# One decoder layer on one core: weight addresses worked out ahead, a shorter inverse root, and a redrawn timetable

## What is computed

```
x = layernorm(x + causal_linear_attention(x))      # 16 heads of 64, 128 random features, exp(x.W - |x|^2/2)
x = layernorm(x + differential_cross_attention(x, ctx))   # 32 half heads of 8, 77 context tokens
x = layernorm(x + experts(x))                      # 16 experts of 128, 4 chosen per token in 2 of 4 groups, and 1 shared
layernorm(x) = (x - mean) / sqrt(var + 1e-5)
```

## Time and profile before

| | |
|---|---|
| median of 3 runs | 789.55 us (783.31 to 789.67) |
| the profiled execution, its own time | 784.78 us |
| its span, from the first to the last instruction | 782.1 us |
| mean granted TensorE clock | 0.986 of full speed |
| PE busy | 731.6 us, 94% of the span |
| DVE busy | 546.0 us, 70% |
| ACT busy | 433.7 us, 55% |
| POOL busy | 273.8 us, 35% |

### The profile page before, as it was taken

How to read it: one execution, slowest core, us unless ns; L and a number is a source line. 1 busy time by engine, 2 the same in 40 slices (tenths; PEclk the granted TensorE clock), 3 DMA queues, 4 the chain that set the end, 5 groups by cost and what they waited for, 6 DMA issues and landing times.

```text
span 782.1 us, 24288 instructions
## 1 busy us (share of the span) xinstructions
PE 731.6 (94%) x9544; PEld 508.8 (65%) x9544; DVE 546.0 (70%) x1549; ACT 433.7 (55%) x880; POOL 273.8 (35%) x320
## 2 busy tenths in 40 slices
PE   5979999999999999999999999998799999999983
PEld 2547666756676776567667756776677787775643
DVE  8477755369546686865758599448989558943887
ACT  4867776264756534567565354753146766664331
POOL 7222112011232110625311054230265255556872
PEclk9999999999999999999999999999989999999997
DMA  8335676424000000311300041043686225424461
GB/s 281 141 95 155 189 149 162 126 54 127 2 3 2 3 2 19 120 41 45 95 2 3 2 156 55 9 165 136 210 272 188 64 92 171 147 82 161 141 208 56
DMA packets 55181, 80.78 MB, mean 103 GB/s; under 512 B 12576, under 2 KB 43424, under 8 KB 54560
## 3 DMA queue, kind: packets, MB, share of 16 engines
q1 hardware_dynamic: 48416, 62.71, 26.3%
q0 software_dynamic: 5376, 15.47, 5.1%
q10 hardware_dynamic: 1280, 1.05, 0.5%
HBM read 42.65 MB, written 33.41 MB: 97 GB/s over the span
## 4 chain that ended last, share of the span: by engine, by line
PE 65%; DVE 25%; issue 3%; ACT 2%; DMA 2%; SPq 1%; POOL 1%; ACTq 0%; DVEq 0%
PE ps L1657 28%; PE ps L1663 14%; PE ps L1755 7%; PE ps L1736 3%; PE ps L1880 3%; DVE xmax L1519 3%; PE ps L1771 3%; DVE st L1328 2%; DVE rows L1345 2%; PE ps L1799 1%; PE ps L1772 1%; DVE root_a L1337 1%; SPq L766 1%; PE ps L1944 1%; DVE attn_mem L1485 1%
## 5 line engine op out<-in xcount | busy, mean ns | idle before, releaser
L968 POOL TENSOR_TENSOR qk<-square,qk 128x512 f16<-128x512 f32 x64 | 75.8, 1186 | 258.9 <-ACT qk L1060 258.8
L1657 PE MATMUL ps<-x_split,w_qkv 128*128 128x512 f16 x384 | 93.8, 382 | 2.9 <-DVE qk L1481 1.9
L1663 PEld LDWEIGHTS ps<-attn_mem 128*64 128x64 f32 x1920 | 78.6, 138 | 24.0 <-issue 21.3
L1663 PE MATMUL ps<-attn_mem 128*64 128x65 f32 x1920 | 93.3, 226 | 0.3 <-issue 0.2
L990 POOL DMA_INDIRECT rows_out<-attn_mem,dest x64 | 62.5, 977 | 41.3 <-ACT attn_mem L1161 26.7
L983 POOL DMA_INDIRECT rows_in<-rows,slot_i x48 | 47.5, 989 | 73.3 <-DVE slot_i L1418 61.2
L1481 DVE SCALAR_TENSOR_TENSOR qk<-ps,qk 128x512 f16<-128x512 f32 x64 | 43.8, 684 | 41.8 <-ACT square L1057 41.6
L1063 ACT ACTIVATE attn_mem<-ps 128x512 f32<-128x512 f32 x64 | 37.7, 595 | 62.1 <-PE ps L1736 62.0
L1101 ACT ACTIVATE prob<-ps 128x512 f32<-128x512 f32 x96 | 52.9, 603 | 21.5 <-PE ps L1663 12.2
L1657 PEld LDWEIGHTS ps<-x_split,w_qkv 128*128 128x128 f16 x384 | 37.1, 98 | 37.7 <-issue 3.9
L1657 PE MATMUL ps<-attn_mem,w_qkv 128*128 128x128 f16 x512 | 55.8, 223 | 3.2 <-DVE attn_mem L1585 2.5
(11 more groups left out here) (307 smaller groups left out, 1872.7 us busy)
## 6 DMA issues: line engine op xcount, KB each, us to landing
attn_mem<-rows_in SPq DMA_DIRECT2D x64, 144.0 KB, 2.4
late_mem<-ffn_w SPq DMA_DIRECT2D x17, 384.0 KB, 3.6
rows_in<-zero_row SPq DMA_DIRECT2D x32, 144.0 KB, 4.8
up_split<-late_mem SPq DMA_DIRECT2D x16, 256.0 KB, 2.8
x_stage<-xT SPq DMA_DIRECT2D x4, 512.0 KB, 5.7
down_split<-late_mem SPq DMA_DIRECT2D x16, 128.0 KB, 2.8
rows<-x SPq DMA_DIRECT2D x4, 512.0 KB, 6.9
xq<-late_mem SPq DMA_DIRECT2D x32, 64.0 KB
```

Of the source, the lines that this page charges most:

```text
L968: pool.tensor_tensor(parts[:, 3, :], square[:, n % 2, :], parts[:, 2, :], ALU.subtract).then_inc(p_sql.sem, 1)
L1657: ins = pe.matmul(dst, lhs(i), rhs(j), start=first and n == 0, stop=last and n == 2)
L1663: ins = pe.matmul(dst[at:at + COLS, :], lhs[:, at:at + COLS], rhs, start=start, stop=stop)
```

## The change

Three things change.

1. PE works out weight addresses ahead of their use. "tile turn" loads the table and puts the 16 addresses of its pair's "tile up" weights on a list (`unaddressed`). After each product of `three_pass` outside "tile up", each transpose of "tile turn", each step of block 3's scores and each product of "probs", `address_ahead` takes one address from the list and has it computed. "tile up" drops what is left of its own and of earlier pairs and computes it where it is used. "tile down" forms its addresses as an expert's byte offset plus a base.
2. `inverse_root` has nine linked instructions instead of twelve: the shift is folded into the first guess, and two Newton steps of second order and third order stand for three of second order.
3. All constants of the timetable are new, the offsets of the engines and the bank holding times too.

```
-ATT = dict(project=(-2.394, -1.514), turn_keys=(2.018, 2.44), q_features=0.94, k_features=0.945,
+ATT = dict(project=(-2.397, -1.539), turn_keys=(2.004, 2.284), q_features=0.91, k_features=0.944,
...
-             dispatch=22.637, keep=35.532, ends=27.727, dispatch_d=0.271)
+             dispatch=22.919, keep=33.392, ends=29.062, dispatch_d=0.114)
...
-HOLD = dict(values=0.478, project=0.75, turn_keys=0.423, q_features=0.397, state=0.595, attend=0.594,
+HOLD = dict(values=0.615, project=0.705, turn_keys=0.635, q_features=0.453, state=0.572, attend=0.527,
...
-           sums_d=1.144, sums_n=0.742, early=-3.569, early_d=1.039, late=5.66, late_d=1.031, pack=-2.023)
+           sums_d=1.139, sums_n=0.634, early=-3.561, early_d=1.048, late=5.674, late_d=1.034, pack=0.189)
...
-    gpsimd=dict(project=0.29, weigh=-1.098, dispatch=-0.9, tile_down=-0.681, combine=-2.003, dense_keep=-0.444,
-                weigh_last=-2.512),
+    gpsimd=dict(project=0.53, weigh=-0.71, dispatch=-1.182, tile_down=-2.911, combine=-2.044, dense_keep=-0.39,
+                weigh_last=-4.65),
...
                 link(dve.tensor_scalar(v, mv[:, :, 1], LN_EPS, None, ALU.add))
-                link(dve.tensor_scalar(a.bitcast(I32), v.bitcast(I32), 1, None, ALU.logical_shift_right))
-                link(dve.tensor_scalar(r.bitcast(I32), a.bitcast(I32), -1.0, float(0x5F3759DF), ALU.mult, ALU.add))
-                for _ in range(3):
-                    link(dve.tensor_tensor(a, r, r, ALU.mult))
-                    link(dve.scalar_tensor_tensor(a, a, -0.5, v, ALU.mult, ALU.mult))
-                    link(dve.scalar_tensor_tensor(r, a, 1.5, r, ALU.add, ALU.mult))
+
+                link(dve.tensor_scalar(r.bitcast(I32), v.bitcast(I32), -0.5, float(0x5F3759DF), ALU.mult, ALU.add))
+
+                link(dve.tensor_tensor(a, r, r, ALU.mult))
+                link(dve.scalar_tensor_tensor(a, a, -0.5 * 0.375, v, ALU.mult, ALU.mult))
+                link(dve.scalar_tensor_tensor(r, a, 1.5 * 0.375, r, ALU.add, ALU.mult))
+                link(dve.tensor_tensor(a, r, r, ALU.mult))
+                link(dve.scalar_tensor_tensor(a, a, 64 / 9, v, ALU.mult, ALU.mult))
+                link(dve.scalar_tensor_tensor(a, a, -10 / 3, a, ALU.add, ALU.mult))
+                link(dve.scalar_tensor_tensor(r, a, 5.0, r, ALU.add, ALU.mult))
...
+            def byte_of(b, n, j, width):
+                return pe.snap(expert_of[b, n, j] * (2 * width))
+
+            def up_weights(b, n, j, part, k, a):
+                first = 2 * (D * k + P * part)
+                return e_bytes[a][:, bass.ds(byte_of(b, n, j, GU) + first, 2 * P)].bitcast(F16)
+
+            def down_weights(b, n, j, a):
+                return d_bytes[a][:, bass.ds(byte_of(b, n, j, D), 2 * D)].bitcast(F16)
+
+            def address_ahead():
+
+                if unaddressed:
+                    pe.lower_ap(unaddressed.popleft()(), for_matmul_weights=True)
+
+            def three_pass(dst, lhs, rhs, first=True, last=True, ahead=True):
 
                 for n, (i, j) in enumerate(((0, 0), (0, 1), (1, 0))):
                     ins = pe.matmul(dst, lhs(i), rhs(j), start=first and n == 0, stop=last and n == 2)
+                    if ahead:
+                        address_ahead()
                 return ins
...
+                    while unaddressed and unaddressed[0].args[1] <= n:
+                        unaddressed.popleft()
                     for j in range(2):
-                        at = pe.snap(expert_of[b, n, j] * (2 * GU))
                         for part in range(2):
                             for k in range(KD):
                                 m = KD * j + k
-                                first = 2 * (D * k + P * part)
                                 last = three_pass(bank[:, 2 * P * part + P * j:2 * P * part + P * j + P],
-                                                  lambda a: e_bytes[a][:, bass.ds(at + first, 2 * P)].bitcast(F16),
-                                                  lambda a: xgT[:, i % 3, a, P * m:P * m + P], k == 0, k == KD - 1)
+                                                  lambda a: up_weights(b, n, j, part, k, a),
+                                                  lambda a: xgT[:, i % 3, a, P * m:P * m + P], k == 0, k == KD - 1, False)
```

More of the change, by code:

```diff
@@ L1 @@
 import itertools
+from collections import deque
 from contextlib import ExitStack
+from functools import partial
 import numpy as np
@@ L117 @@
-MISC = dict(keys=3.411, tail=8.014, setup=1.455, setup_d=0.979, load_x=3.099, split_x=-4.602, load_stream=8.241,
-            experts_0=-6.556, experts_1=-3.498, rows_in=-2.106, up=1.797, down=4.371)
+ATT = dict(project=(-2.397, -1.539), turn_keys=(2.004, 2.284), q_features=0.91, k_features=0.944,
+           attend=(1.761, 3.758), state=(2.697, 3.71), output=(3.718, 4.667), turn_output=5.579, values_0=2.035,
+           values_1=0.095)
+CHAIN = dict(first=3.585, first_d=0.296, out=3.822, out_d=0.124, norm1=4.455, turn=5.065, queries=5.599, scores=6.487,
+             scores_d=0.077, maxima=9.427, probs=9.919, probs_d=0.118, norm2=13.642, cross=15.275, gate=15.822,
+             route0=16.089, up=16.389, route1=18.529, route2=19.696, down=17.08, route3=19.7, prefix=21.998,
+             dispatch=22.919, keep=33.392, ends=29.062, dispatch_d=0.114)
@@ new lines @@
+CHAIN_2 = dict(first=3.358, first_d=0.409, out=3.813, out_d=0.273, norm1=4.884, turn=5.611, queries=5.812,
+               scores=6.986, scores_d=0.055, maxima=9.324, probs=9.953, probs_d=0.115, norm2=14.088, cross=15.41,
+               gate=17.227, route0=17.235, up=18.013, route1=18.25, route2=19.181, down=19.566, route3=19.533,
+               prefix=20.058, dispatch=14.958, keep=19.669, ends=20.223, dispatch_d=0.309)
+HOLD = dict(values=0.615, project=0.705, turn_keys=0.635, q_features=0.453, state=0.572, attend=0.527,
+            turn_output=0.61, k_features=0.672, output=0.546, project_out=0.573, turn_stream=0.951, queries=0.819,
+            scores=0.631, turn_maxima=0.901, probs=0.551, weigh=0.666, turn_cross=1.378, gate=1.06, shared_up=1.569,
+            shared_down=2.669, prefix=0.578, pack=2.553, weights=0.756, tile_turn=1.201, tile_up=1.02,
+            tile_down=1.493, dense_gate=0.505, dense_up=2.697, dense_weigh=2.753)
@@ L121, in schedule @@
+MISC = dict(keys=6.832, tail=8.292, setup=0.909, setup_d=1.015, load_x=1.404, split_x=-3.754, load_stream=11.123,
+            experts_0=-7.69, experts_1=-5.301, rows_in=-1.611, up=1.751, down=4.284)
 def schedule():
@@ L218, in chain_jobs @@
             put(start + at["ends"], "table", 0, 1)
[L222 to L225, removed]
-           sums_d=1.144, sums_n=0.742, early=-3.569, early_d=1.039, late=5.66, late_d=1.031, pack=-2.023)
+END = dict(first=-4.562, first_d=0.943, out=-3.312, out_d=0.191, norm1=0.048, turn=-0.212, queries=0.274,
+           scores=-0.296, scores_d=0.244, maxima=7.759, probs=8.889, probs_d=0.137, norm2=16.756, cross=19.297,
+           gate=19.448, route0=19.786, up=21.87, route1=21.391, route2=22.532, down=23.756, route3=24.733,
+           weights=26.377, dense=26.844, dense_d=2.132, dense_2=1.336, pick=1.418, keep=1.879, sum=6.474, sums=36.876,
+           sums_d=1.139, sums_n=0.634, early=-3.561, early_d=1.048, late=5.674, late_d=1.034, pack=0.189)
 def tile_time(k):
@@ L330 @@
[L330 to L337, removed]
+    sync=dict(rows_in=-0.809, setup=0.172, load_x=6.556, load_stream=6.415, load_context=-0.033, queries=0.975,
+              queries_last=1.262, keep=-0.799, experts=-0.156, ends=3.162, fetch=-1.663),
@@ L1940, in _ @@
                     pe.wait_ge(*xg_loaded[i % XG](i // XG + 1, 0))
+                    if 2 * n in (0, EARLY):
+                        pe.wait_ge(*table_ready(0, 1 if n == 0 else 2))
+                    if 2 * n % LOADED == 0:
+                        t = (TILE_BASE[b] + 2 * n) // PER_E
+                        four = loaded(mybir.EngineType.PE, expert_i[0:1, t:t + LOADED // PER_E], 16 ** PER_E - 1)
+                        for m in range(LOADED):
+                            expert_of[b, n + m // 2, m % 2] = four[m // PER_E] // 16 ** (m % PER_E) % 16
+                    for j in range(2):
+                        for part in range(2):
+                            for k in range(KD):
+                                for a in range(2):
+                                    unaddressed.append(partial(up_weights, b, n, j, part, k, a))
                     for j in range(2):
```

37 lines of the change are left out of this document (19 added, 18 removed).

## The result

The kernel after takes 773.24 us (median of 4 runs, 772.56 to 774.12), the kernel before, run beside it, 788.25 (4 runs, 783.31 to 789.67). The measured ratio is 0.9848, with a 95% interval of 0.9809 to 0.9889: 12 us on 789.55, where 7.9 were forecast. The profiled execution went from 784.78 to 774.12 us, 10.7 us, forecast 776.9. Both came out faster than the forecast. The median is close to rival A's 773.6, but A's gain was 16 us, counted from a median of 789.55 that was high; the measured gain lies between the forecast's and A's.

A forecast was written before the change was run, and what follows sets the result against it. PE was taken to bound the attention stage, DVE the stretch from 528 to 580 us. Addresses -2.7, inverse root -5.2 and timetable 0 gave -7.9 us: profiled 784.78 to 776.9 us, range 771 to 792.

The forecast's parts named there:

- rival A: Tile up steps: addresses are free, every step takes 1.34 us; -16 us in all, 773.6; chance 0.22 with a lucky timetable.
- Two of my own signs of being wrong: Tile-only turns falling to 2.5 us, or the stage before 500 us moving by more than 4 us.
- Addresses, -2.7: PE's tile pairs: 2.7 us won where long products stood; tile-only turns stay about 3.0 us.
- Rival E: PE's addresses: nothing of them shows, only the roots count; -5.2 us, 784.3; chance 0.08.
- Norm3 of block 1, -2.0: DVE's chain there: `shift` ends at 755.74 instead of 757.77, 2.0 us, all of it reaching PE.
- my fear that the three POOL instructions would find the shorter chain all the same: Norm3 of block 1: if the same three POOL instructions fell in, the term would be 0.6 us, not 2.0.
- The other norms, -3.2 together: Last norm 0.6 us, norm3 of block 2 0.6, of block 0 0.3, three norms in blocks 2 and 3 1.8.
- the other five: Norms in chains of earlier blocks, beside attention products: 0, or 0.6 us each if that cover is thinner.
- The constants, 0: Redrawn timetable and `HOLD`: most moves small or hidden, sign of the bank times unknown, taken as 0.
- Rival C: Attention stage: new `HOLD` puts a head's products on a bank whose reader is not done; slower, 797.7; chance 0.14.
- B: Norms: the roots are hidden; left are 0.6 us at the end and 1 us of addresses; 788.0; chance 0.17.
- D: Address list: does nothing, addresses are computed again where used; 20 to 40 us slower; chance 0.03.

The follow-up runs named there:

- root in norm3 only: Kernel before with the nine-step inverse root in the four norm3 only, twelve steps in norm1 and norm2: 780.76 us, ratio 0.9966.
- root alone: Kernel before with the nine-step `inverse_root` in all norms as the only change: 775.35 us, ratio 0.9876.
- the kernel after with fence: Kernel after, with POOL made to wait for norm3's shift before the additions of the next block's second combine: 773.85 us, ratio 0.9890.
- with fence and plain gate: Kernel after, with POOL waiting for norm3's shift before the second combine's additions and no addresses worked out in gate jobs: 769.49 us, ratio 0.9837.

## Why the prediction was right, and where it was off

Direction and range held. The sum was 4 us short by the ratio and 2.8 by the profiled executions, and the terms were off by more than that, in both directions: in the order root, addresses, constants the parts gave 9.7, 1.7 and 0.5 us, where I had 5.2, 2.7 and 0. That the sum came as near is in part luck. The median of 773.24 us also lies below the forecast's own 777 to 786, in the part of the range that I had given to A or a lucky timetable. Two of my own signs of being wrong came close or true without their rivals: the turns fell to 2.7 us (A said 2.5), and at block 3's first features, before 500 us, the time had moved by 5.3 us, more than the 4 us of C, but the other way.

- **Addresses, -2.7.** Measured 0.9 to 1.7 us with the old constants, 4.7 to 6.7 with the new. The price of a register instruction, 0.114 us, was right (0.112), but by luck: the step of 1.82 us that I divided by 16 holds 14 of them. The step that failed is that 16 addresses a pair need a place outside the up step and find only 10, so that the tile-only turns stay at 3.0 us: an up step hides ten by itself. I had counted what it holds and not what it can hold, though the nine clean steps of before showed it. The turns went to 2.7 us. Also, the change does remove instructions: 450 in line 1677 and 103 in line 1682 make 553, against 640. The other half of the idea, that the work moves and is paid for elsewhere, was right, but I looked for the place in transposes and down steps and never priced the gate, with its 24 products 0.025 us apart. Rival E is out: the addresses do show, with the new constants at least. Rival A was right about the step of 1.34 us and wrong that it is free.
- **Norm3 of block 1, -2.0.** The wait went to 1.46 us, forecast 1.6, and the stretch gave 3.7 us. DVE's chain got 2.0 us shorter, as forecast, though in the kernel before four of its steps were held up and not three. The step left out is the clock: PE's half speed in 3.1 us of work behind the wait. The 1.03 us for two products at the end of the earlier trace rows had shown it. And my fear that the three POOL instructions would find the shorter chain all the same was the wrong question: with nine steps there is a race with a DMA, worth up to 5.3 us in this stretch. The Trainium skill ("SBUF — State Buffer", section "Who interferes with whom") has the rule for who is locked out, and the traces agree again: 1.19 us beside a POOL instruction of 1.26.
- **The other norms, -3.2 together.** Root everywhere minus root in norm3 only is 7.1 us (about 4 to 10 by the intervals), of which at most 1.8 had been put on norm1 and norm2. The cover over "the other five" was thinner than PE's waits showed; the alternative that I gave, 0.6 us for each, would have come closer. The trace of root alone shows 2.9 us of the 7.1: PE's waits from 500 to 700 us sum to 10.7 us, before 13.6. Which norms give the rest stays open. Those that POOL does not touch run 0.6 us shorter, as forecast, but the last one only 0.4: 1.99 us up to its first scaling, before 2.39.
- **The constants, 0.** Right for the change as a whole (0 and -0.5 us beside the addresses), wrong as a statement about themselves (+3.7), and "idle within 2 of 12 us" is wrong: it fell to 8.7 us (484.00 - 475.32 in the window of after). Rival C's bank waits did not show. B is out by PE's wait at norm3, D by the count of 553.

## What to carry to other kernels

Before moving work out of a step, ask how much of it the step hides where it stands, and read that from the instances that already run at full pace; only the excess has to move. Then check every place that the moved work may land in, by the length of the shortest product there: here one exception for a job of 16-column products was worth 4.4 us, about a third of the whole change. A wait of an engine whose clock can fall costs more than its length, so look at the clock of the window behind it.

## What was not expected of the hardware

- At the end of PE's wait of 3.65 us the granted clock fell to 0.50, and 3.1 us of work behind it ran at that clock; around one of 1.46 us it stayed 1.00 [before and after, norm3 of block 1].
- With the same waits of PE before it, 1.5 to 1.6 us twice, the clock went from 1.00 to 0.50 inside a gate whose 24 products of 16 columns start mostly 0.112 us apart, and stayed at 1.00 where they start 0.025 us apart [the kernel after with fence, with fence and plain gate; one trace each].
- A 4-column DVE instruction of 0.16 us took up to 1.19 us beside POOL, and in the one trace that has it a start 0.03 us ahead of POOL's was enough to escape.
- Between register instructions in PE's stream there are never less than 0.11 us, though most are recorded at 32 ns; behind products that start 0.025 us apart they set the pace of the products.
